# Rope attentions: inverse softmax sums by a block turn and a trip through DRAM, in place of GpSimd widening and TensorE turns

## What is computed

```python
q, k, v = rope(x @ Wq), rope(x @ Wk), x @ Wv          # per head
s = q @ k.T * scale                                   # causal mask
p = exp(s - max(s)); sums = p.sum(-1)                 # per query row
y = (p @ v) / sums                                    # softmax, normalised late
out = sum over heads of y @ Wo
```

## Time and profile before

| | us |
|---|---|
| median of 3 runs | 1811.53 (1811.27 to 1812.1) |
| span of the profiled execution | 1790.1 |
| a2 (stretch from 570 to 855) | 285, TensorE busy 275.33 |
| h2 (stretch from 900 to 1285) | 385, TensorE busy 384.33 |
| TensorE busy in the whole span | 1648.9 |

### The profile page before, as it was taken

One profiled execution on the slowest core, in us unless ns is written; L12 is line 12 of the kernel. 1 busy time (PEld: TensorE's weight loads), 2 busy tenths in 40 slices (PEclk: granted clock), 3 DMA queues, 4 the chain that ended last, 5 costly groups with the idle time before them and its releaser, 6 DMA issues. The chain is left out here.

```text
span 1790.1 us, 28231 instructions
## 1 busy us (share of the span) xinstructions
PE 1648.9 (92%) x9295; PEld 1084.2 (61%) x9313; DVE 1022.1 (57%) x2123; ACT 1016.1 (57%) x2184; POOL 766.4 (43%) x715
## 2 busy tenths in 40 slices
PE   5899998787998999999799999999989999978998
PEld 3567653355995566666455555555448887434786
DVE  5856675632224555555356655556458887662675
ACT  4534554553324555555466666656538887754786
POOL 1235533016343566666265565555324442121363
PEclk8999998999999999999999999999989999989999
DMA  1008232001223222222211111111036652000430
GB/s 42 2 15 193 59 112 93 1 1 37 76 71 106 60 60 60 60 59 48 77 42 49 43 42 47 40 46 45 16 106 239 223 216 99 2 0 21 138 114 26
DMA packets 61865, 124.69 MB, mean 70 GB/s; under 512 B 14258, under 2 KB 29477, under 8 KB 55228
## 3 DMA queue, kind: packets, MB, share of 16 engines
q1 hardware_dynamic: 59580, 119.24, 22.7%
q0 software_dynamic: 2144, 3.70, 0.7%
HBM read 79.05 MB, written 11.02 MB: 50 GB/s over the span
## 5 line engine op out<-in xcount | busy, mean ns | idle before, releaser
L1993 ACT ACTIVATE h_probs<-psum,h_nmax 128x512 f32<-128x512 f32 (+3 forms) x256 | 133.1, 526 | 127.4 <-DVE h_nmax L2073 69.8
L2073 DVE TENSOR_REDUCE h_nmax<-psum 128x1 f32<-128x512 f32 (+3 forms) x256 | 116.2, 486 | 103.1 <-PE psum L1877 103.0
L917 ACT ACTIVATE psum<-psum,f_b 128x512 f32<-128x512 f32 x200 | 132.3, 662 | 30.0 <-PE psum L874 30.0
L1802 POOL TENSOR_TENSOR h_swapped<-h_swapped,rope_tables 128x512 f32<-128x512 f32 x64 | 81.8, 1279 | 152.4 <-DMA h_swapped<-h_raw 152.4
L840 POOL TENSOR_TENSOR e_lo<-e_gated,e_hi 128x512 fp32r<-128x512 f32 x59 | 76.1, 1291 | 148.3 <-ACT e_hi L929 148.3
L126 PE MATMUL psum<-rope_tables,mean_w 128*128 128x256 f32 x490 | 124.0, 404 | 14.9 <-DMA slots<-f_rows,f_slots 8.2
L1993 ACT ACTIVATE a_probs<-psum,a_nmax 128x512 f32<-128x512 f32 (+3 forms) x128 | 67.4, 527 | 121.7 <-DVE a_nmax L2073 73.3
L1802 POOL TENSOR_TENSOR a_swapped<-a_swapped,a2f_a_tables 128x512 f32<-128x512 f32 x64 | 81.7, 1276 | 122.5 <-DMA a_swapped<-a_raw 122.4
L952 DVE TENSOR_TENSOR e_lo<-psum,e_hi 128x512 fp32r<-128x512 f32 x168 | 114.7, 683 | 25.0 <-ACT psum L917 25.0
L126 PEld LDWEIGHTS psum<-rope_tables,mean_w 128*128 128x128 f32 x490 | 96.9, 203 | 38.0 <-issue 21.5
L872 PE MATMUL psum<-f_x_hi,f_w_hi 128*128 128x512 f32 x272 | 107.5, 395 | 3.6 <-DVE e_gated L966 2.6
(11 more groups left out here) (492 smaller groups left out, 4165.1 us busy)
## 6 DMA issues: line engine op xcount, KB each, us to landing
e_gate<-gates SPq DMA_DIRECT2D x39, 1024.0 KB, 4.7
a_swapped<-a_raw SPq DMA_DIRECT2D x128, 128.0 KB, 2.3
h_swapped<-h_raw SPq DMA_DIRECT2D x256, 64.0 KB, 2.0
e_gate<-gates SPq DMA_DIRECT2D x16, 512.0 KB, 7.4
f_w<-in_l_experts SPq DMA_DIRECT2D x32, 128.0 KB, 4.7
slots<-a_empty SPq DMA_DIRECT2D x1, 2600.0 KB, 7.6
f_w<-in_l_experts SPq DMA_DIRECT2D x9, 256.0 KB, 4.9
e_got<-slots SPq DMA_DIRECT2D x7, 325.0 KB, 4.8
```

Source lines behind the costliest of these rows:

```text
L917: nc.scalar.activation(to, hidden_bank(n), ex.act_func, **bias(n)).then_inc(act_ready, 1)
L1802: nc.gpsimd.tensor_tensor(swapped[:, j, :], swapped[:, j, :], tables[:, 2 * j + 1, :], ALU.mult).then_inc(sin_ready, 1)
L1993: nc.scalar.activation(probs[:, j % 4, 0:(q + 1) * P], ring[j % RING][:, 0:(q + 1) * P], ACT.Exp, bias=nmax[:, j % 8:j % 8 + 1], accum_out ...
L2073: nc.vector.tensor_reduce(nmax[:, j % 8:j % 8 + 1], ring[j % RING][:, 0:(q + 1) * P], AX.X, ALU.max, negate=True).then_inc(max_ready, 1)
```

## The change

The widening, the TensorE turns and ScalarE's copy go away. After the reciprocal, VectorE turns the 128x32 block of inverses in blocks of 32x32, so that one inverse row stands along the free dimension. SP stores it to a DRAM tensor `inverses` and loads it back into `r_sb`, spread over the partitions of each head (one load in a2, two in h2). `rsum` and `rinv` get a layout of 32 columns per unit, `r_sb` two buffers, and `normalise` waits for the load. `project_q` no longer waits for the copy of the sums. A memset on GpSimd clears the unused columns once per stage.

```diff
 @block.sync
+                def store_inverses(U):
+                    sp.wait_ge(turned, U + 1)
+                    sp.dma_start(inverses[U % 4].rearrange("j p i -> p j i"), rinv_t[:, U % 2, :]).then_inc(inverses_stored[U % 2], 16)
+                def spread_inverses(U):
+                    sp.wait_ge(inverses_stored[U % 2], 16 * (U // 2 + 1))
+                    if U >= 2:
+                        sp.wait_ge(y_ready, U - 1)
+                    for h in range(heads):
+                        sp.dma_start(r_sb[h * dv:(h + 1) * dv, U % 2, :],
+                                     inverses[U % 4, h * QT:(h + 1) * QT].rearrange("q p i -> (q p i)").partition_broadcast(dv)).then_inc(inverses_loaded[U % 2], 16)
                 for V in range(NU):
+                    if V > AHEAD:
+                        store_inverses(V - AHEAD - 1)
                     for j in range(2):
                         sp.wait_ge(raw_ready[j], V + 1)
                         if V >= 1:
                             sp.wait_ge(qk_ready, 2 * V - 1 + j)
                         for lo, hi in halves:
                             sp.dma_start(swapped[hi:hi + half, j, :], raw[lo:lo + half, j, :]).then_inc(swap_loaded[j], 16)
+                    if V > AHEAD:
+                        spread_inverses(V - AHEAD - 1)
+                for U in range(NU - AHEAD - 1, NU):
+                    store_inverses(U)
+                    spread_inverses(U)
 @block.gpsimd
+                nc.gpsimd.memset(rinv[:], 0.0).then_inc(zeroed, 1)
-                    if V > AHEAD:
-                        widen(V - AHEAD - 1)
 @block.tensor
-                    if V >= 4:
-                        pe.wait_ge(r_copied, V - 3)
-                    for q in range(QT):
-                        last = nc.tensor.transpose(misc[0][:, q * P:(q + 1) * P], rinv_wide[:, q * P:(q + 1) * P], core.ident[:])
 @block.scalar
-                    nc.scalar.activation(r_sb[:], misc[0], ACT.Copy).then_inc(r_copied, 1)
 @block.vector
+                def turn_inverses(U):
+                    dve.wait_ge(rinv_ready, U + 1)
+                    if U >= 2:
+                        dve.wait_ge(inverses_stored[U % 2], 16 * (U // 2))
+                    nc.vector.transpose(rinv_t[:, U % 2, :], rinv[:, U % 2, :]).then_inc(turned, 1)
                 def normalise(U):
-                    dve.wait_ge(r_copied, U + 1)
+                    dve.wait_ge(inverses_loaded[U % 2], 16 * heads * (U // 2 + 1))
-                    nc.vector.tensor_tensor(y[:, U % 2, :], misc[1], r_sb[:], ALU.mult).then_inc(y_ready, 1)
+                    nc.vector.tensor_tensor(y[:, U % 2, :], misc[1], r_sb[:, U % 2, :], ALU.mult).then_inc(y_ready, 1)
```

More of the change, by code:

```diff
@@ L1748, in rope_attention @@
         nmax = st.sb("nmax", [P, 8])
-        rsum, rinv = (st.sb(n, [P, 2, QT, heads]) for n in ("rsum", "rinv"))
-        rinv_wide, r_sb = (st.sb(n, [P, T]) for n in ("rinv_wide", "r_sb"))
+        rsum, rinv, rinv_t = (st.sb(n, [P, 2, 32]) for n in ("rsum", "rinv", "rinv_t"))
+        r_sb = st.sb("r_sb", [P, 2, T])
+        inverses = core.dram["inverses"]
         y = st.sb("y", [P, 2, T])
@@ L1755, in rope_attention @@
         (proj_ready, v_psum, v_ready, prep_psum, prep_done, sin_ready, qk_ready, s_ready, max_ready, probs_ready,
-         pt_psum, copied_dve, copied_act, rinv_ready, wide_ready, r_psum, r_copied, values_done, y_ready, out_done, sum_done) = (st.sem(n) for n in (
+         pt_psum, copied_dve, copied_act, rinv_ready, turned, values_done, y_ready, out_done, sum_done) = (st.sem(n) for n in (
              "proj_ready", "v_psum", "v_ready", "prep_psum", "prep_done", "sin_ready", "qk_ready", "s_ready",
-             "max_ready", "probs_ready", "pt_psum", "copied_dve", "copied_act", "rinv_ready", "wide_ready", "r_psum", "r_copied", "values_done", "y_ready",
+             "max_ready", "probs_ready", "pt_psum", "copied_dve", "copied_act", "rinv_ready", "turned", "values_done", "y_ready",
              "out_done", "sum_done"))
+        zeroed = st.sem("zeroed")
+        inverses_stored, inverses_loaded = ([st.sem(f"{n}{k}") for k in range(2)] for n in ("inverses_stored", "inverses_loaded"))
         ring = [core.psum[:, k, :] for k in range(RING)]
@@ L1807, in _ @@
                         nc.gpsimd.tensor_tensor(to[:, V % 3, :], rot[:, j, :], swapped[:, j, :], ALU.add).then_inc(qk_ready, 1)
-                for U in range(NU - AHEAD - 1, NU):
-                    widen(U)
             @block.tensor
@@ L1819, in project_q @@
                         pe.wait_ge(x_split, b + 1)
-                    if V >= 4:
-                        pe.wait_ge(r_copied, V - 3)
-                    elif V >= 1 and merged:
+                    if V >= 1 and merged:
                         pe.wait_ge(raw_ready[0], V)
@@ L1905, in values @@
                                 last.then_inc(values_done, 1)
[L1907 to L1915, removed]
-                    for q in range(QT):
-                        last = nc.tensor.transpose(misc[0][:, q * P:(q + 1) * P], rinv_wide[:, q * P:(q + 1) * P], core.ident[:])
-                    last.then_inc(r_psum, 1)
                 def out(U):
@@ L1940, in between @@
                         if slot == 4:
-                            spread_sums(U - 1)
                             values(U - 1, (1,))
@@ L1993, in exponential @@
                         nc.scalar.activation(probs[:, j % 4, 0:(q + 1) * P], ring[j % RING][:, 0:(q + 1) * P], ACT.Exp,
-                                             bias=nmax[:, j % 8:j % 8 + 1], accum_out=rsum[:, U % 2, q, h:h + 1]).then_inc(probs_ready, 1)
+                                             bias=nmax[:, j % 8:j % 8 + 1], accum_out=rsum[:, U % 2, h * QT + q:h * QT + q + 1]).then_inc(probs_ready, 1)
                 def copy_t(K):
@@ L2040, in _ @@
                         round_x(U)
-                    if n == 2 and U >= 1:
-                        copy_sums(U - 1)
-                copy_sums(NU - 1)
             @block.vector
@@ L2086, in inverse_sums @@
                     dve.wait_ge(probs_ready, per_unit * (U + 1))
+                    if U == 0:
+                        dve.wait_ge(zeroed, 1)
                     if U >= 2:
-                        dve.wait_ge(wide_ready, U - 1)
-                    nc.vector.reciprocal(rinv[:, U % 2, :, :], rsum[:, U % 2, :, :]).then_inc(rinv_ready, 1)
+                        dve.wait_ge(turned, U - 1)
+                    nc.vector.reciprocal(rinv[:, U % 2, 0:per_unit], rsum[:, U % 2, 0:per_unit]).then_inc(rinv_ready, 1)
+                def turn_inverses(U):
[3 more added lines that the diff above has]
+                    nc.vector.transpose(rinv_t[:, U % 2, :], rinv[:, U % 2, :]).then_inc(turned, 1)
                 def normalise(U):
                     dve.wait_ge(values_done, heads * (U + 1))
-                    dve.wait_ge(r_copied, U + 1)
+                    dve.wait_ge(inverses_loaded[U % 2], 16 * heads * (U // 2 + 1))
                     if U >= 2:
                         dve.wait_ge(out_done, U - 1)
-                    nc.vector.tensor_tensor(y[:, U % 2, :], misc[1], r_sb[:], ALU.mult).then_inc(y_ready, 1)
+                    nc.vector.tensor_tensor(y[:, U % 2, :], misc[1], r_sb[:, U % 2, :], ALU.mult).then_inc(y_ready, 1)
                 def add_out(b):
@@ L2140, in _ @@
                         inverse_sums(U - 1)
+                        turn_inverses(U - 1)
                     if n == 0 and U >= 2 and (U - 1) % G == 0:
@@ L2155, in _ @@
                 inverse_sums(NU - 1)
+                turn_inverses(NU - 1)
                 normalise(NU - 1)
@@ L3143 @@
     dram["slots"] = nc.dram_tensor("slots", (EXPERTS * CAPACITY, ROW), F32, kind="Internal").ap()
+    dram["inverses"] = nc.dram_tensor("inverses", (4, 32, 4, 32), F32, kind="Internal").ap()
     dram["homes"] = nc.dram_tensor("homes", (2 * N, P), F32, kind="Internal").ap()
```

## The result

The changed kernel takes 1943.63 us (median of 4 runs, 1942.92 to 1949.68) against 1811.40 for the kernel before (4 runs, 1810.43 to 1812.10): a ratio of 1.074, 95% interval 1.072 to 1.076, or 132 us more. The prediction was 1913 us, range 1848 to 1955, slower with a chance of 0.93. The sign, the mechanism and the place were right; the size was 30 us low.

A forecast was written before the change was run, and what follows sets the result against it. The prediction took TensorE to bound both attentions, with a late load then setting each unit's period. It added 38 us in a2, 57 in h2 and 7 at the ends to 1811.5, giving 1913 us, range 1848 to 1955.

The forecast's parts named there:

- The bound and the sign: Both rope attentions run at TensorE's pace with dependency chains nearly touching it; the change makes them slower, chance 0.93.
- TensorE's gain: Removing the turns frees 0.44 us of TensorE per unit in a2 and h2, at most 27 us in all.
- The loop in a2: From y through swaps and load to the next y: 10.29 us against 8.98, +1.31 per unit, 38 us over 29 units.
- the store's delay: On SP in a2, the store issued ahead of the swaps makes them start 0.2 us late.
- The loop in h2: From y through eight swaps and two loads to y: 14.35 us against 12.38, +1.97 per unit, 57 us over 29 units.
- the clock: Granted clock stays at 1.00 in both stages; a fall while TensorE waits for y was named as a danger outside the range.
- the upper ends of its landings: Loads landing in 3.5 us in a2 and 3.6 in h2, which would give 1934 us.
- the slow store: Rival: a2's store lands in 4.0 us, later than the covered 2.86, on four engines; 1952 us, chance 0.15.
- The ends: The bare store and load path at the stage ends adds 5 us in a2 and 2 in h2.
- What lies around the span: The median's 21.4 us above the profiled execution's 1790.1 us span, carried over unchanged to the forecast.
- Cheap loads: Rival: spread loads land like plain ones, 2.6 us in a2 and 2.1 in h2; 1858 us, chance 0.2.
- Faster: Rival: the loop through the load doesn't close, so only TensorE's 0.44 us per unit remains; 1791 us, chance 0.05.

The follow-up runs named there:

- The run without the wait: Changed kernel with y multiplied by a table in SBUF, so VectorE waits for the inverse loads only at the last unit: 1791.15 us, ratio 0.986.
- the run with the early inverse and the load first: Changed kernel with inverse and turn ahead of the previous unit's y, and store and loads on SP ahead of the next unit's swaps: 1784.98 us, ratio 0.987.
- the control: Kernel before, widening and TensorE turns kept, with its inverse sums put ahead of the y of the unit before: 1811.11 us, ratio 1.000.

## Why the prediction was right, and where its size was off

**The bound and the sign.** Read rightly: both stages ran at TensorE's pace, with chains close under it, so a longer chain would set the period. The run without the wait shows that all of the loss enters there.

**TensorE's gain.** 8.54 and 11.94 us were worked out from two weight loads 0.44 us apart; 8.54 and 11.95 were measured, in four of the runs for h2 and in three for a2.

**The loop in a2.** Forecast 10.29: 4.56 to the first swap with the store's delay, 2.43 for the swaps, 3.3 for the load and the wake-up. The unit shown has 4.62, 2.52 and 3.68. The load is the term that was mis-sized most: e_gate's first load with its 3.2 us was one in a quiet queue; this one goes out behind four swaps of 128 KB and lands in 3.4 (median), and 3.5 pass from its issue to y (median). In the run with the early inverse and the load first, where nothing is queued right ahead of it, it lands in 3.2. The prediction had that danger as the upper end of its bound, 3.5. The store's delay was mis-sized as well: its issue takes 0.57 us and not the 0.33 of e_gate's first load, and it holds up the swaps by 0.40 (4.62 less 4.22) and not by 0.2. The rest of that stretch, told as 4.36, is 4.22, which hides most of it.

**The loop in h2.** Forecast 14.35; the unit shown has 14.01, and the median with the clock held is 14.04. The two loads take 3.62 to y and not 3.9: they land in 2.9 (median) and not in the 3.2 of the earlier trace rows.

**The step that failed: the clock.** The sum carried the granted clock of 1.00 in the earlier trace rows over to a kernel in which TensorE waits 2 us in every unit. The danger was named, and left outside the sum and the range. With the clock held by idle-time matmuls, the first 28 periods are longer than those of the kernel before by 46.6 us in a2 and 51.7 in h2, 98 in all, where the prediction has 38 + 57 = 95: a2 too low and h2 too high cancel. Without them it is 54.4 and 64.0. So the dips cost 20 us in these periods, and the count unit by unit gives 19.6; by the times of the two kernels it is 26 to 29. Of the 30 us that were missing, 20 are the dips, 2 the loops with their ends, and 8 stay unplaced.

**The range.** It held, but not for its reason. With the forecast's mechanism and the upper ends of its landings the prediction has 1934 us, and 1943.63 lies above that. The range reached to 1955 for the slow store, which the runs refute; what filled that room was the clock, which the prediction had put outside. That part is luck.

**The ends.** The last three periods of a2 are 5.9 us longer than before (+5 told), those of h2 0.3 (+2 told).

**What lies around the span.** This was wrong without harm. The prediction took 1811.5 less 1790.1, 21.4 us, as lying around the span. In every timed run here time and span differ by about 2 us (1942.92 and 1941.0, for one); the profiled execution of the kernel before was a short one (1790.1, where its later timed runs span 1803 us or more). Part of that can be placed: its first y in a2 comes at 587.85 us, in the later runs between 596 and 605, mostly in code that no version touches. Its a2 and h2 are the usual ones (273.5 and 373.2 us; the control has 274.5 and 373.2), so the sum stood.

**The rivals.** Cheap loads: refuted, 3.4 and 2.9 us where 2.6 and 2.1 were wanted. The rule of the Trainium skill, "DMA: Bandwidth & Descriptors", section "Anatomy of one DMA" (about 2.0 us plus the bytes at 436 GB/s; estimates of 2.6 and 2.3 us), which is fitted for the GpSimd path, is 0.6 to 0.8 us short of these spread loads on SP's queue; the measurement decides. Slow store: refuted. With nothing in between, the load leaves 1.99 us after the store's issue in both stages, well within the 2.86 that the swaps cover. The Trainium skill, same page, section "Why a DMA increments its semaphore by 16 and not by 1", would put this store on four engines. The trace agrees as far as it goes: each of the 64 stores of the changed kernel ends in four packets of 4 B, where a load of h2's inverses ends in 16, and once the store is under way four of its packets start every 9 to 10 ns. They are through within 0.36 us (1.20 to 1.56 us after the issue), so four engines are no burden at 16 KB. Faster: the rival asked for an order on SP other than the one written. Such an order alone was not enough in a2 (9.7 us, 1830 us in all); it needed the earlier inverse as well, and then gave 1785, near the 1784 that 27 us less would be.

## What to carry to other kernels

When a step is moved from an engine to a round trip through DRAM, look for what closes a loop over it: a DMA of 3.5 us is free or lengthens every unit, depending on how early its input can be had and what stands ahead of it in its queue. Move the producer to the first point at which its data exist and the DMA ahead of the transfers that don't need to hurry, both together; each alone left 17 or 115 us of loss here. And if an engine that was always busy will wait in every unit, price the drop of its clock too.

## What the runs showed of the hardware

- A load spread from one DRAM row to 128 partitions, 256 KB, lands in 3.2 to 3.5 us (medians of the runs with little queued behind it) and in 3.7 to 3.8 when swaps of 128 KB are issued right behind it; the swaps behind it land in 3.4 in place of 2.3.
- A 16 KB store to DRAM and the wait for it take 1.98 us (median) on SP from issue to the next issue, the same in a2 and in h2. Its packets move only between 1.20 and 1.56 us after the issue.
- On SP the issue of a2's load takes 0.32 us when SP has waited before it and 0.53 behind a burst of swaps; that of the store takes 0.57 though SP has waited before it, and that of a swap 0.59 (medians). Eight swaps of 64 KB hold its queue for 4.96 us, longer than one of them takes to land (2.0 in the median, at most 3.3).
- Idle-time matmuls in a 2 us wait made a kernel 26 us faster, since the granted clock stayed at 1.00 in place of 0.94 to 0.97. In the run with the load ahead of all swaps TensorE waits for y only about 1.2 us in each unit of a2 (39.6 us in 32 waits, the longest 2.5), and the clock there stays at 1.00 with nothing added.
- VectorE's block turn of 128x32 takes 0.21 us, where one of 128x512 takes 0.66.
